# The third term's product ahead of the numerator's backward scan, and the next side load between logarithm and exponential

## What is computed

```python
def cond(r, k, v, w, u, time_emb):        # k = v = side input, r = x
    tf = sigmoid(sum(time_emb))
    decay = exp(-exp(w)) * (0.5 + 0.5 * tf)
    ek = exp(minimum(k, 30)); ekv = ek * v
    nf, df = forward scans of ekv and ek with decay
    nb, db = backward scans of ekv and ek with decay
    euk = exp(minimum(u + k, 30))
    num = nf + nb - ekv + euk * v          # euk * v is the third term
    den = df + db - ek + euk
    return sigmoid(r) * num / maximum(den, 1e-8) * (0.8 + 0.2 * tf)

x = x + linear(cond(x, side, side, w0, u0, c))
h = cond(x, side, side, w1, u1, c)
x = x + h + moe(rmsnorm(h)) + shared_expert(rmsnorm(h))
```

## Time and profile before

| | us |
|---|---|
| median of 3 runs (5141.24 to 5148.24) | 5145.92 |
| the profiled execution's own time | 5147.97 |
| its span, first to last instruction | 5146.2 |
| TensorE busy in the span | 4498.5 (87%) |
| VectorE busy | 2643.4 (51%) |
| ScalarE busy | 1734.7 (34%) |
| units 0 to 7 (alone) | 15.1 to 355.1 |
| units 8 to 31 (fused) | 355.1 to 1842 |

### The profile page before, as it was taken

How to read it: one execution, slowest core, us unless ns; L and a number is a source line. 1 busy time by engine, 2 the same in 40 slices (tenths; PEclk the granted TensorE clock), 3 DMA queues, 4 the chain that set the end, 5 groups by cost and what they waited for, 6 DMA issues and landing times.

```text
span 5146.2 us, 61244 instructions
## 1 busy us (share of the span) xinstructions
PE 4498.5 (87%) x19727; PEld 3561.0 (69%) x19729; DVE 2643.4 (51%) x2813; ACT 1734.7 (34%) x2531; POOL 599.7 (12%) x811
## 2 busy tenths in 40 slices
PE   4447888888888899980999999999999999999998
PEld 1125666666666677760788888788788887888787
DVE  8888878787878745241233134343434134133332
ACT  4444444443444433211223133233323124132332
POOL 0000000000000000046111111111111111111111
PEclk7778999999998999995999999999999999999999
DMA  5554656656656576774345345365555246354442
GB/s 205 209 215 162 227 205 212 208 202 217 211 200 220 199 240 205 173 174 112 103 106 155 65 139 172 108 194 165 172 142 156 57 109 201 61 159 106 135 126 57
DMA packets 268791, 833.89 MB, mean 162 GB/s; under 512 B 48944, under 2 KB 82160, under 8 KB 244080
## 3 DMA queue, kind: packets, MB, share of 16 engines
q1 hardware_dynamic: 193696, 573.10, 33.0%
q0 software_dynamic: 47824, 158.43, 14.6%
q10 hardware_dynamic: 27136, 100.67, 5.3%
HBM read 651.68 MB, written 180.42 MB: 162 GB/s over the span
## 4 chain that ended last, share of the span: by engine, by line
PE 60%; DVE 17%; issue 10%; ACT 6%; DMA 4%; POOL 2%; DVEq 0%; ACTq 0%; SPq 0%; POOLq 0%
PE ps L1339 32%; PE ps L1353 16%; PE ps L1234 7%; PE ps L1320 3%; DMA work<-side_t 2%; DVE work L872 2%; DVE work L860 2%; POOL slots_dram L489 2%; DVE work L863 2%; DVE work L857 1%; DVE work L887 1%; DVE work L885 1%; PE ps L1328 1%; DVE work L867 1%; ACT work L560 1%
## 5 line engine op out<-in xcount | busy, mean ns | idle before, releaser
L1339 PE MATMUL ps<-halves 128*128 128x512 f32 x7152 | 1744.5, 396 | 27.4 <-DVE halves L1148 22.2
L1234 PE MATMUL ps<-halves 128*128 128x512 f32 x6144 | 1506.3, 407 | 119.1 <-DVE work L1023 83.3
L1339 PEld LDWEIGHTS ps<-halves 128*128 128x128 f32 x7152 | 1327.7, 189 | 301.3 <-DVE halves L1148 24.3
L1234 PEld LDWEIGHTS ps<-halves 128*128 128x128 f32 x6144 | 1197.0, 196 | 420.6 <-issue 133.8
L1353 PE MATMUL ps<-halves 128*128 128x512 f32 x3576 | 834.9, 389 | 1.3 <-DVE halves L1157 1.3
L1353 PEld LDWEIGHTS ps<-halves 128*128 128x128 f32 x3576 | 671.2, 188 | 140.7 <-DVE halves L1157 1.5
L1143 DVE TENSOR_TENSOR halves<-ps,halves 128x1024 fp32r<-128x1024 f32 x150 | 183.7, 1225 | 929.6 <-ACT halves L747 929.6
L1148 DVE TENSOR_TENSOR halves<-work,halves 128x1024 fp32r<-128x1024 f32 (+1 forms) x320 | 440.2, 1434 | 111.5 <-ACT halves L756 111.5
L747 ACT ACTIVATE halves<-ps 128x1024 fp32r<-128x1024 f32 x150 | 154.0, 1027 | 988.5 <-PE ps L1339 888.0
L756 ACT ACTIVATE halves<-work 128x1024 fp32r<-128x1024 f32 (+1 forms) x320 | 369.3, 1220 | 99.0 <-PE ps L1353 68.4
L1320 PE MATMUL ps<-ident,work 128*128 128x128 f32 x1200 | 156.2, 273 | 122.2 <-DMA work<-rows_dram,row_idx 122.2
(11 more groups left out here) (159 smaller groups left out, 3815.2 us busy)
## 6 DMA issues: line engine op xcount, KB each, us to landing
halves<-split_dram SPq DMA_DIRECT2D x512, 512.0 KB, 5.1
work<-expert_w SPq DMA_DIRECT2D x192, 1024.0 KB, 5.4
split_dram<-halves ACTq DMA_DIRECT2D x32, 1024.0 KB, 5.6
plain<-shared_w SPq DMA_DIRECT2D x32, 512.0 KB, 4.0
gated_dram<-work ACTq DMA_DIRECT2D x32, 512.0 KB, 3.7
work<-x_t ACTq DMA_DIRECT2D x32, 512.0 KB, 5.1
work<-side_t ACTq DMA_DIRECT2D x32, 512.0 KB, 4.3
ratio_dram<-work ACTq DMA_DIRECT2D x32, 512.0 KB, 3.0
```

The lines of the kernel that those rows point to most:

```text
L1234: last = pe.matmul(bank(k % 4), w, op[:, part], start=(c == 0 and w is w_hi and op is hi), stop=(c == CB - 1 and w is w_lo))
L1339: last = pe.matmul(ps_h[:, a * 512:a * 512 + 512], xp[:, xk * P:(xk + 1) * P], wp[:, rhs], start=(xk == 0 and xp is xhi and wp is whi), st ...
```

## The change

Two instructions move; none is added or removed.

On VectorE, in both passes of each unit, the product W*K (L874 before) moves from behind the backward scan of the numerator (L872) and fill(4l+2) to directly behind the lower bound of the denominator (L869). The scan and fill(4l+2) now come after it; the addition L877 follows fill(4l+2).

On ScalarE, in the second pass, `load_side(u + 1)` moves from behind the exponential into `inverse`, between the logarithm and the exponential. It is still behind fill(6).

```diff
                     sc.activation(N, F, ACT.Ln).then_inc(s["g_ln"], 1)
+                    if l == 1:
+                        load_side(u + 1)
                     sc.wait_ge(s["g_ln"], u * 2 + l + 1)
                     sc.activation(N, N, ACT.Exp, scale=-1.0).then_inc(s["g_inv"], 1)
...
                 inverse(1)
-                load_side(u + 1)
                 fill(7)
...
                     ve.tensor_scalar(F, F, low[:, at], None, ALU.max).then_inc(s["den"], 1)
+                    ve.scalar_tensor_tensor(W, W, cap[:, at], K, ALU.min, ALU.mult).then_inc(s["wv_done"], 1)
                     ve.wait_ge(s["nf"], n + 1)
                     ve.wait_ge(s["n_edge"], n + 1)
                     ve.tensor_tensor_scan(G[:, ::-1], d, G[:, ::-1], edge_in[:, 1:2], ALU.mult, ALU.add).then_inc(s["nb"], 1)
                     fill(4 * l + 2)
-                    ve.scalar_tensor_tensor(W, W, cap[:, at], K, ALU.min, ALU.mult).then_inc(s["wv_done"], 1)
                     ve.wait_ge(s["nb"], n + 1)
                     ve.wait_ge(s["wv_done"], n + 1)
                     ve.tensor_tensor(G, G, W, ALU.add).then_inc(s["num"], 1)
```

## The result

| | before | changed | ratio, 95% interval |
|---|---|---|---|
| median of 6 runs each (us) | 5147.08 | 5164.89 | 1.0039 (1.0029 to 1.0049) |
| lowest to highest | 5141.24 to 5153.38 | 5160.24 to 5168.74 | |
| profiled execution, own time | 5147.97 | 5164.32 | |

The change costs 17.8 us by the medians and 16.4 by the two profiled executions; the interval of the ratio is 15 to 25 us. The forecast was +21.8.

A forecast was written before the change was run, and what follows sets the result against it. Half the last-ending chain is TensorE's expert tiles, untouched; in the fused units neither VectorE nor TensorE is full, so their order decides. -4.6 + 22.6 + 2.0 + 1.8 = +21.8 us on 5145.9 gives 5167.7; range 5154 to 5178.

The forecast's parts named there:

- First pass: Fused units: the early product delays L885 by 1.19 us through the gapless ScalarE chain; 19 passes, 22.6 us lost.
- Quarter 2: Fused first passes: the product hides in L1029's wait for TensorE, no cost, except unit 10, which loses 1.2 us.
- Units alone: Units 0 to 6, second pass: load leaves 2.27 us earlier; 4.6 us gained, bounds nothing to 15.4.
- if the load stands in line behind the stores of its own queue, all that it gains is the holes: Units alone: with transfer engines full at 393 GB/s, the load lands 0.65 us earlier; seven units give 4.6.
- rival A: Units alone: the load overtakes, sharing engines with the stores from issue; 15.4 us gained, total 5156.9; chance 0.18.
- Second pass, quarters 0 to 2: Fused units: load and clip come a net 0.11 us later in 18 units, 2.0 us lost.
- now it leaves 0.15 after the logarithm starts: Fused second pass: load issue 1.08 us earlier in the stream, logarithm 1.19 later, so net 0.11 later.
- the waits for the load in quarters 0 to 2 would shrink: Sign in the fused units' profile: if these waits, about 68 us, shrink, the prediction is wrong.
- Second pass, quarter 3: Fused units: L1044 and the clip net later, average 0.3 us in six units, 1.8 us lost.
- B: Fused first pass: slack of 1.2 us in the ScalarE chain, so no delay; about 5143; chance 0.05.
- C: Everywhere the load leaves when L874 ends; 68 us of waits go, total 5085; sign L570 ahead of L603; chance 0.05.
- D: Clips of quarters 0 to 2: load shifted against SyncE's loads costs 0.5 us each, 9 us, total 5177; chance 0.10.

The follow-up runs named there:

- experiment 12: The changed kernel, unaltered, measured again: 5160.98 us, 1.0035 of the kernel before.
- experiment 1: Changed kernel with the first pass's product put back behind the scan and fill(4l+2), early in the second pass only: 5145.06 us, 0.9998.
- experiment 7: Changed kernel plus a second VectorE operation of the product's size ahead of the numerator's scan in the first pass: 5187.04 us, 1.0086.
- experiment 5: Changed kernel with the side load of alone units 0 to 6 issued from SyncE's queue instead of ScalarE's: 5163.52 us, 1.0038.
- experiment 9: Changed kernel with the two split stores of fill(5) issued at fill(7), behind the side load, in alone units 0 to 6: 5149.76 us, 1.0012.
- experiment 3: Kernel before with only the load moved between logarithm and exponential, both products left in place: 5138.47 us, 0.9985.
- experiment 6: Changed kernel with both moves kept in alone units 0 to 6 only, the order before in all others: 5142.93 us, 1.0000.
- experiment 11: Kernel before with only the two split stores of fill(5) moved behind the load, in alone units 0 to 6: 5145.03 us, 1.0005.
- experiment 4: Changed kernel with the product early in the second pass only and the side load moved ahead of fill(6) on ScalarE: 5100.29 us, 0.9911.

## Why the prediction was right, and where it was off

**First pass: right in place, sign and size.** 1.19 us were predicted for each of 18 units, and 17 of them show 1.18 to 1.21, the other 0.91; experiment 12 repeats it. Experiments 1 and 7 show the cause from both sides: without the early product the loss goes, with a second operation it doubles. The wait came in two parts, L1091 and L886, and not in one as forecast. The first is the product with the sigmoid, behind the first half of the same ScalarE chain. In quarter 3 the wait is ahead of L1045, where it was forecast.

**Quarter 2: right.** TensorE's lateness covers the product (-0.9 over five units), and unit 10, which has no such cover, pays 0.74 (forecast 1.2).

**Units alone: size and reason off, and the sign not clear of the spread.** The 4.6 came from the step "if the load stands in line behind the stores of its own queue, all that it gains is the holes". The gain was 3.0, 1.7 and 0.8 in three profiles and nothing in a fourth. That the load gains little while the stores stand ahead is right, and rival A is out. But the order of its own queue isn't needed for that: experiment 5 gave it another queue and it waited as long. Experiment 9 shows the cause, the stores issued ahead; behind the load they cost little. So all seven units still waited 2.0 us each at the clip, where 1.5 was forecast. And the size was worked out from a rate that doesn't hold; the same stretch in the changed kernel (columns as in the earlier trace rows) shows:

```profile
90.00:91.00 1.00, 0.00 (x0) 0.00 (x0) 0.98 (x1) 0.00 (x0) 0.00 (x0) 0.50 0.98 213
91.00:92.00 1.00, 0.00 (x0) 0.00 (x0) 0.00 (x0) 0.00 (x0) 0.00 (x0) 0.50 0.96 393
92.00:93.00 1.00, 0.00 (x0) 0.00 (x0) 0.11 (x1) 0.00 (x0) 0.00 (x0) 0.50 0.32 127
```

At 90 the engines are busy for 0.98 of the time and move only 213 GB/s. I had taken "busy" for 393 GB/s. Where the load goes first it is much the same: in experiment 9, at 87:88, ScalarE's queue moves 0.28 MB in that microsecond at a share of 91.3%, and no other queue moves anything.

The rule of ring order in the Trainium skill (DMA: Bandwidth & Descriptors, section on queues, rings and completion order), which the forecast set beside its 4.6, binds only within one queue, so it doesn't explain experiment 5. The same section says that an engine takes its queues in turn, but drains a whole packet, typically some 9 to 17 descriptors, before it switches. By estimate a store of 1 MB is 16 of the profile's packets of 4 KB on each of the 16 engines; if those are the descriptors meant, it could be one such piece. The 90:93 window of experiment 5 agrees with that reading: ScalarE's queue had moved 1.07 MB at 87:90, which is the first store, the load could start at 90.5 at the earliest (1.0 us after its issue, as in experiment 9), and by then the second store was running. No run here shows where an engine switches, so the rule is not shown as the cause.

**Second pass, quarters 0 to 2: the step failed that says "now it leaves 0.15 after the logarithm starts".** In quarter 0 the load leaves with the logarithm's start, in quarters 1 and 2 some 0.3 us before it: the issue overtakes the queued activation. So the move up the stream was worth 1.2 to 1.5 us and not 1.08, as experiment 3 shows by itself. Against the delay of 1.19 the load leaves sooner than before in all 18 units, by 0.01 to 0.33 us (1.08 in unit 10), 5.0 us together, where +2.0 was forecast. The two profiles show +0.75 and -4.4. The +3.55 of quarter 0 in the first isn't shown to be an effect of the change, since experiment 12 has -1.03 there.

The forecast named as a sign against it that the waits for the load in quarters 0 to 2 would shrink. They did, from 68.1 to 65.6 us and to 60.3 in experiment 12, and the failed step is why they could: the load leaves a little sooner and not 0.11 later. But the spread is as large, since with the fused order of before experiments 6 and 11 have 74.0 and 69.2. The waits that the main term stands on appeared as forecast.

**Second pass, quarter 3: right** (+1.6 for +1.8).

**Not foreseen: -3.5 from the clip to the next unit.** It is mostly at two turns of the loop in quarter 3 (units 19 and 27, 1.71 each), where VectorE's first instruction has no releaser in the profile. First the kernel before, then experiment 6:

```profile
DVE work L1023 <- issue: 13.1, 4, 5.1
DVE work L1033 <- issue: 9.5, 4, 3.3
```

In the changed kernel the same wait (L1024) has 9.7 in four. But experiment 6 has the fused units in the order of before and shows 9.5, and experiment 11, also in that order, 13.4. So the shorter wait comes without the change in the fused units too, and isn't shown to be its effect; what decides it stays open.

**The sum is nearer than its parts.** The expert stage is unchanged, as forecast. The medians' 17.8 are 4 below the 21.8. The first pass alone gives 21.0 of the 22.6 forecast; the small terms around it partly cancel, and they are no larger than the spread between profiles.

**The rivals.** B fell with experiments 1 and 7. C as a forecast of this change was rightly set low: the load stood behind fill(6), and experiment 4 shows that this was what held it. Its sign was badly chosen: L570 did start ahead of L603, by 0.3 us in quarters 1 and 2, and yet it left 4 to 5 us behind the product. And its price was too good. The 5085 holds the 22.6 us of the first pass, which experiment 4 doesn't pay; without them it would be 5062, and 5100 was measured. In its trace quarters 0 to 2 gain 50.5 of the 68 us in the second pass, since a load issued 5 us sooner took about 2 us longer, 9.3 go back between the clip and the next unit, and the units alone gain 1.5 and not 15.4. D (9 us more by shifted loads) didn't show: the second passes of quarters 0 to 2 change by +0.75 and -4.4. Two sums of the rivals are slightly off by their own terms: A's "+11.0" is 10.8 (15.4 - 4.6), which its 5156.9 has right, and B's "about 5143" is 5145 with the 3.8 of the second pass.

**Left open:** why the other queue's packets start only when the second store has drained; why the load takes longer in the fused stage when it leaves sooner (7.5 us for 6.57 in unit 17), for which company by SyncE's transfers is only argued; and what decides the wait at the turn of the loop.

## What to carry to other kernels

Before an operation moves ahead of a block of queued work, look up what another engine waits for in that block. A chain that runs through a second engine and back without a gap passes the whole microsecond on, in every unit. A transfer issued sooner keeps its head start only if nothing large stands ahead of it: move the small, urgent load ahead and the bulk store behind it, and measure the two together. Here the early load alone gave the units alone 0 to 3 us, the stores' move alone gave nothing (1.0005), and both together gave 13. With the load ahead of fill(6) and the first pass's product left in its place, that made 0.9875. And profile a kernel twice before a difference of a few microseconds between two traces is explained: here two profiles of one kernel differed by 5 us in one term.

## What the runs showed of the hardware

- In experiment 5 transfers of two queues ran one after the other: a 0.52 MB load, issued at 89.53 on a queue of its own, had no packet between 90 and 93, while 0.97 MB of another queue's stores passed. In none of the seven units did such a load's first packet come sooner than 3.1 us after its issue. It isn't so everywhere: in unit 17 of the kernel before, at 936.5:937.5, SyncE's queue moved 0.25 MB and ScalarE's, with the load, 0.14.
- With nothing of its queue ahead, a load's first packet came 1.0 us after its issue (experiment 9, units 0 to 6).
- A transfer in ScalarE's stream can leave before an activation that stands ahead of it has started, by 0.30 us (935.41 against 935.71), if it doesn't wait for that activation.
- A busy share of the transfer engines of 0.98 went with 213 GB/s at one place and 0.96 with 393 in the next microsecond. The share alone doesn't tell how much moves.
- The profile's "issue" can hide a true releaser: the 0.74 us ahead of L886 end 0.09 after ScalarE's exponential, and stay 0.75 when the whole chain is later by another microsecond.
